# Squares folded to two tiles by VectorE before each variance, and the channel mix added to the residual by one accumulating DMA

## The reference, cut to what matters

```
cond:   y = sigmoid(x) * num / den * (0.8 + 0.2 tf)    # num, den: scans over the 512 tokens in both
                                                      # directions, keys and values from fside
attn:   h  = layernorm(y)                      # mean and variance over the 512 channels
        r, k, v = mixes of h and its shifted copy, each @ (512 x 512)
        x1 = y + (sigmoid(r) * wkv(k, v)) @ Wout
        h2 = layernorm(x1)                     # second mean and variance
        r2 = sigmoid(mix(h2) @ cWr);  k2 = relu(mix(h2) @ cWk) ** 2
        x2 = x1 + r2 * (k2 @ cWv)              # the channel mix added to the residual
x = x + x2
x = x + ffn(cond2(x))     # cond2: the same scans, gated by the new x; ffn: shared expert and 32 routed experts, top 8
```

## Time and profile before

| | |
|---|---|
| median of 3 runs | 1136.41 us (1134.61 to 1138.21) |
| the profiled execution's own time | 1126.11 us |
| its span | 1124.4 us |
| TensorE busy | 1048.5 us, 93% of the span |
| VectorE busy | 724.5 us, 64% |
| ScalarE busy | 513.0 us, 46% |
| GpSimd busy | 472.0 us, 42% |

### The profile page before, as it was taken

The page is one execution under the profiler, slowest core; times in us unless marked ns, Lnnn a source line. Parts: engine busy times, 40 slices in busy tenths (PEclk is TensorE's granted clock), DMA queues, the critical chain, the costliest instruction groups (busy, mean ns, idle before and its releaser), DMA issues.

```text
span 1124.4 us, 13091 instructions
## 1 busy us (share of the span) xinstructions
PE 1048.5 (93%) x4094; PEld 649.4 (58%) x4095; DVE 724.5 (64%) x1346; ACT 513.0 (46%) x778; POOL 472.0 (42%) x432
## 2 busy tenths in 40 slices
PE   0479999999999999999999999998999999999788
PEld 0344444444444444554644444446999999999788
DVE  8998449999999999870787000003555555555376
ACT  4465525656565556341221111113666666666211
POOL 3533003532353236220008777662666666666500
PEclk9999999999999999999999999999999999999889
DMA  4563024432643211321204685357766776677398
GB/s 149 173 213 101 1 38 138 151 101 59 204 151 101 64 39 33 101 38 75 75 1 139 216 286 191 143 174 205 161 157 157 157 156 157 157 157 157 115 405 299
DMA packets 186322, 157.23 MB, mean 140 GB/s; under 512 B 113824, under 2 KB 159392, under 8 KB 184224
## 3 DMA queue, kind: packets, MB, share of 16 engines
q1 hardware_dynamic: 170336, 113.12, 35.6%
q0 software_dynamic: 15936, 43.53, 12.3%
HBM read 67.09 MB, written 68.55 MB: 121 GB/s over the span
## 4 chain that ended last, share of the span: by engine, by line
PE 75%; DVE 17%; issue 4%; DMA 2%; ACT 1%; POOL 0%; ACTq 0%; POOLq 0%; SPq 0%; DVEq 0%
PE banks L1596 24%; PE banks L605 13%; PE banks L616 12%; PE banks L570 10%; PE banks L543 10%; PE banks L675 2%; PE banks L519 2%; DMA arena<-parts 2%; DVE arena L1345 2%; PE banks L1611 2%; DVE arena L1336 2%; DVE arena L1334 1%; DVE arena L1447 1%; DVE arena L1438 1%; PE banks L665 1%
## 5 line engine op out<-in xcount | busy, mean ns | idle before, releaser
L1596 PE MATMUL banks<-arena 128*128 128x512 f32 x896 | 389.7, 595 | 12.2 <-DVE arena L1399 5.1
L1596 PEld LDWEIGHTS banks<-arena 128*128 128x128 f32 x896 | 170.3, 191 | 228.7 <-issue 216.9
L482 POOL DMA_INDIRECT parts<-arena x160 | 171.0, 1069 | 126.4 <-DVE arena L879 101.3
L474 POOL DMA_INDIRECT slots_in<-arena x128 | 129.2, 1010 | 91.1 <-issue 87.1
L605 PEld LDWEIGHTS banks<-arena 128*128 128x128 f32 x1280 | 156.8, 194 | 7.9 <-issue 3.9
L605 PE MATMUL banks<-arena 128*128 128x128 f32 x1280 | 157.4, 277 | 3.0 <-ACT arena L713 3.0
L616 PE MATMUL banks<-arena 128*128 x640 | 151.1, 379 | 0.0
L879 DVE TENSOR_TENSOR arena<-banks,arena 128x512 f32<-128x512 f32 x80 | 55.3, 691 | 119.9 <-PE banks L616 119.9
L616 PEld LDWEIGHTS banks<-arena 128*128 128x128 f32 x640 | 115.6, 190 | 12.5
L543 PE MATMUL banks<-arena 128*128 128x512 f32 x256 | 114.3, 592 | 0.0
L570 PE MATMUL banks<-arena 128*128 128x512 f32 x256 | 114.1, 592 | 0.0
(11 more groups left out here) (179 smaller groups left out, 1239.7 us busy)
## 6 DMA issues: line engine op xcount, KB each, us to landing
slots_in<-arena SPq DMA_DIRECT2D x20, 1120.0 KB, 5.9
arena<-parts SPq DMA_DIRECT2D x16, 1024.0 KB, 10.0
arena<-fT SPq DMA_DIRECT2D x32, 256.0 KB, 2.8
arena<-w2T SPq DMA_DIRECT2D x4, 2048.0 KB, 13.6
arena<-xT SPq DMA_DIRECT2D x4, 1024.0 KB, 7.9
arena<-xT POOLq DMA_DIRECT2D x4, 1024.0 KB, 9.7
arena<-w1T SPq DMA_DIRECT2D x2, 2048.0 KB, 13.1
out<-arena SPq DMA_DIRECT2D x16, 256.0 KB, 6.9
```

The lines of the kernel that those rows point to most:

```text
L474: pool.indirect_dma_start(rows_in, bass.IndirectOffsetOnAxis(ap=POSU[:, n, j:j + 1], axis=0), XLR[:, n].bitcast(mybir.dt.uint32), None).th ...
L482: pool.indirect_dma_start(parts, bass.IndirectOffsetOnAxis(ap=DESTU[:, g:g + 1], axis=0), YO[:, i % 4, c], None).then_inc(y_sent[i % 4], 16)
L1596: ins = pe.matmul(out, w[:, k, m * P:(m + 1) * P], x[:, k], start=(k == 0), stop=(k == kt - 1))
```

## The change

Two things are changed.

1. Six of the eight variances (all four of the second layer norm, those of batches 2 and 3 of the first) get a `fold` ahead of them: one VectorE instruction adds squares tiles 2 and 3 to tiles 0 and 1 (128 x 1024 elements), and TensorE then multiplies two tiles and not four. TensorE waits for `sq{which}_folded` there and no longer for ScalarE's squares.
2. For batches 0, 1 and 2 the four instructions of `x_new` are gone from VectorE. GpSimd issues one accumulating DMA from `R2S` to `XN[:, b]` (1 MB, from SBUF to SBUF) ahead of its work for slot 7, once `final_a` is done, and ScalarE's `sig_new` waits for the DMA's semaphore `x_full`. Batch 3 keeps `x_new`.

```diff
+        def folded(which, b):
+            return which == 2 or b >= 2
...
                 for n, it in enumerate(items):
...
+                    if b is not None and n == 7:
+                        new_x(b - 1)
                     if nx is not None and not last:
                         mid(nx)
                     post(it)
...
-                if b is not None:
-                    pool.wait_ge(S['x_summed'], 16 * b)
+            def new_x(b):
+
+                pool.wait_ge(S['x_summed'], 16 * (b + 1))
+                pool.wait_ge(S['v2_evac'], 4 * b + K)
+                pool.dma_start(XN[:, b], R2S, accum_op=ALU.add).then_inc(S['x_full'], 16)
...
             def sig_new(b):
                 for m in range(K):
-                    act.wait_ge(S['xnew_ready'], 4 * b + m + 1)
+                    act.wait_ge(*((S['x_full'], 16 * (b + 1)) if b < B - 1 else (S['xnew_ready'], m + 1)))
...
+            def fold(which, b):
+
+                dve.wait_ge(S[f'sq{which}_ready'], b + 1)
+                sq = squares(which, b)
+                dve.tensor_tensor(sq[:, 0:2], sq[:, 0:2], sq[:, 2:4], ALU.add).then_inc(S[f'sq{which}_folded'], 1)
...
                 def open_second():
                     if b >= 2:
                         x_side(b - 2, 3)
+                    if b == 1:
+                        fold(2, 0)
                     product(b, 0)
                     normalise(2, b - 1)
...
                     center(1, b + 1)
+                    slot(items[6], lambda: fold(1, b + 1))
                 else:
                     slot(items[5])
-                slot(items[6])
+                    slot(items[6])
...
-                x_new_all(b - 1)
                 if nxt:
                     slot(items[7], settle_second)
+                    fold(2, b)
                 else:
...
                     bonus_num(it)
+                    fold(2, b)
                     x_sides(b - 1)
...
             def var(which, b):
                 src = squares(which, b)
-                pe.wait_ge(S[f'sq{which}_ready'], b + 1)
-                for k in range(K):
-                    ins = pe.matmul(STAT, ones, src[:, k], start=(k == 0), stop=(k == K - 1))
+                if folded(which, b):
+                    pe.wait_ge(S[f'sq{which}_folded'], folds(which, b))
+                else:
+                    pe.wait_ge(S[f'sq{which}_ready'], b + 1)
+                n = K // 2 if folded(which, b) else K
+                for k in range(n):
+                    ins = pe.matmul(STAT, ones, src[:, k], start=(k == 0), stop=(k == n - 1))
```

More of the change, by code:

```diff
@@ L208, in squares, with folds @@
             return MR if which == 1 and b != 1 else NR
+        def folded(which, b):
+            return which == 2 or b >= 2
+        def folds(which, b):
+            return b + 1 if which == 2 else b - 1
         def bank(n):
@@ L221, in build @@
             z2_ready sq2_ready mean2_done var2_done rs2_ready norm2_ready own2_ready mix2_ready mix_columns shifts_ready
+            sq1_folded sq2_folded
             r_mm k_mm v_mm o_mm r2_mm k2_mm v2_mm
             r_evac k_evac v_evac o_evac r2_evac k2_evac k2_ready v2_evac
-            x_summed
+            x_summed x_full
             xnew_ready xnew_sig xs_ready xs_stored0 xs_stored1
```

## The result

The changed kernel takes 1146.13 us (median of 5 runs, 1143.07 to 1148.84), beside 1137.79 us (1134.61 to 1138.21) of the kernel before in the same job: ratio 1.0073, 95% interval [1.0047, 1.0100]. It is slower by some 8 us. Forecast were 1135.9 us, in a range that ends at 1141.0.

The account below looks back on a forecast made before the run. A cycle's chain alternates between VectorE's piece (63.5 us) and TensorE's (48.5 us). Entry -1.42, cycles -0.26 and exit +1.14 sum to -0.5 us: 1136.41 becomes 1135.9 us, range 1131.5 to 1141.

Parts of the forecast that it names:

- The entry: Second norm of batch 0: VectorE waits for TensorE's variance there, so two matmuls fewer gain 1.42 us; its fold is free.
- The price of a fold: Each fold on VectorE was taken at 1.14 us, from the nearest row, L1438, of the same size.
- rival 1: TensorE is the bound by its sum, so all 10.3 us of removed matmuls are saved: 1126.1 us; chance 0.07.
- The fold went first and GpSimd was stopped: At both places in a slot the fold starts first; GpSimd gives up to 1.1 us, VectorE later by as much.
- The DMA was hidden in both cycles: DMA taken to land 9.7 us after issue, under 16 us of cover in a cycle, so it costs nothing.
- a sign of being wrong: ScalarE waiting for `x_full` at the exit would show the forecast wrong; the DMA's cover there was put at 12.2 us.
- The two cycles: VectorE's piece loses `x_new` (2.41 us) and gains two folds (2.28 us): -0.13 us a cycle, -0.26 us for two.
- One place can give something back: GpSimd's L1011 may stop the third of VectorE's L1474, losing up to 0.5 us of lead: +0.35 a cycle, not -0.13.
- rival 4: GpSimd stops each of five folds outside the entry by some 0.9 us: +4.5 us, 1140.4 us; chance 0.11.
- count for nothing in the sum: Matmuls removed from four variances in VectorE's piece of two cycles only lengthen TensorE's wait for L1399: no gain.
- my own forecast for the wait: TensorE's wait for L1399 in each cycle was to grow from 1.72 to about 3.6 us.
- The exit: Iteration 3: the fold ahead of `x_sides` lies on VectorE's chain and counts in full, +1.14 us (to +1.7).

Follow-up runs that it names:

- fold_only: The changed kernel without the DMA: the six folds stay and `x_new` is back on VectorE; cycles of 117.01 and 115.30 us.
- fold_early: The changed kernel with the second norm's fold moved ahead of the slot's second backward scan; 1142.7 us, ratio 1.0049 to the kernel before.
- fold_before_num: The changed kernel with the second norm's fold one instruction earlier, in front of L1377, which releases GpSimd; cycles of 111.82 and 113.43 us.
- best: The kernel before plus the DMA and only second-norm folds, in front of L1377, none at the exit; ratio 0.9987 [0.9959, 1.0016].
- early_padded: fold_early with four matmuls of each cycle issued twice, about 3.4 us of TensorE; stretch 3.5 us shorter than in fold_early.
- second_padded: second_only with four matmuls of each cycle issued twice, 3.4 us of TensorE; 1127.26 us beside 1130.66 us of second_only in the same job.
- second_only: fold_early without the first norm's folds and without the fold at the exit; 1130.66 us.

## Why the prediction was wrong

**What held.** The entry, -1.42 us, to the hundredth. The price of a fold, 1.13 us. The removed matmuls lay where TensorE waits for VectorE, so rival 1 did not come. The fold went first and GpSimd was stopped. The DMA was hidden in both cycles. At the exit ScalarE did wait for it (8.56 us to 470.99 us), which I had named as a sign of being wrong; but ScalarE then waited 5.22 us more for VectorE before the squares, so it cost nothing. What I looked for was a wait where I should have looked for a late successor.

**The step that failed first: "The two cycles", with its "One place can give something back".** I followed one collision with GpSimd, L1011 against the three L1474, and bounded it at 0.5 us; it cost 0.39. There were two more on the same stretch. The prediction had the fold stop GpSimd, "with VectorE later by as much", and took that for no cost; but GpSimd became 0.91 us later and VectorE 1.13, and this slip of 0.22 us let GpSimd's third operation stop the 128 x 2 operation (+1.00). Then L1011 of the next slot, released behind VectorE's late clip, stops the fourth L1474 (+1.11). The term was +2.09 a cycle and not -0.13. fold_only, fold_early and fold_before_num show that the fold's place makes the stop of L1352; the stop of L1494 stands in the two kernels that have the stop of L1352 (the changed one and fold_only) and in none of the others, and no experiment parts the two. "The folds are stopped by GpSimd" (rival 4) was the right fear with the wrong victim: the folds take 1.22 us in every profile and were never stopped.

**The step that failed second: the removed matmuls "count for nothing in the sum".** They are idle time of TensorE, and the clock fell behind it. In the profiles 104 records take 44.90 us behind waits of 0.28 to 1.72 us, 44.90 or 46.60 behind 1.99 to 2.00 us, and 46.46 to 47.89 us behind 3.19 to 3.24 us. The stretch of 152 at the exit takes 65.50 us up to a wait of 2.00 us, and 67.06 to 68.41 behind 3.19 us, in all six kernels that have such a wait. So one long wait ahead of TensorE's piece costs 1.6 to 3.0 us, about as much as the two matmuls that a fold removes (1.72 us) or more. The trace of before had a row that warned, outside the stretch that I read: up to 70 us TensorE is busy for only 23.36 us, so the two engines are both nearly full from 200 us on and not from the start. At 74.22 us its products start behind a wait of 4.71 us, and the window behind it stands at half clock:

```profile
74.22 32.84 PE L1596 MATMUL banks<-arena 128*128 128x512 f32 x72 [4.71 <-DVE arena L1450]
```

```profile
76.00:78.00 2.00, 2.00 (x3) 0.68 (x2) 2.00 (x5) 2.00 (x4) 0.00 (x0) 0.50 0.11 31
```

The waits of 1.7 us left the clock at 1.00, and my own forecast for the wait was 3.6 us, between the two. It should have been priced from both. The Trainium skill, page "TensorE: Matmul & The Clock Gate", section "Part 1: The HAM clock gate (the "warmup" mystery)", says that the half-rate clock is the default and that recent activity lifts it, and that it varies from run to run where the change falls. By this rule equal waits can end in either clock, and the trace agrees: 1.99 and 2.00 us in best, and 2.99 us at the exit with and without a loss. early_padded against fold_early, and second_padded against second_only, are the direct tests: matmuls added, VectorE's work unchanged, and stretches 3.5 and 3.4 us shorter. In time the second pair shows it, 3.4 us in one job with intervals apart; the first pair's 2.8 us are from two jobs with intervals that overlap.

**The exit.** The fold's +1.14 was right. The clock made it 2.4 us in this profile. Of the five kernels with this fold and a wait of 2.99 to 3.00 us behind it, four lose clock there (7.64 to 7.78 us for 24 records) and fold_before_num does not (6.09 us).

**The sum.** Forecast were -0.5 us. In the profile the path to the channel mix gained 1.42 and lost 4.18 in the cycles, 1.14 for the last fold, and 1.55 + 1.26 to the clock: +6.7. The medians differ by 8.3 us, with an interval of 5.3 to 11.4 us.

**What stays open.** Why the clock falls behind one wait of 2.0, 2.1 or 3.0 us and not behind another equal one was not settled in this case; even the profiles of before and after differ at 54 to 66 us, where TensorE's instructions are the same. It is also open why VectorE's small operation gets in ahead of GpSimd's next instruction when it comes 0.28 to 0.30 us before the running one ends, and is stopped for the whole of the next when it comes 0.06 us before; the Trainium skill, page "SBUF — State Buffer", section "Who interferes with whom", gives a lock held for a whole instruction, and the duration of 1.32 us that ends with L1029 agrees. The share of the second part was not worked on; fold_only's stretch is 2.8 us longer than the changed kernel's and its ratio lower, and the second part's scatter is large enough for that.

## What to carry to other kernels

Where two engines take turns as the chain, work removed from one while it waits is not free time: it can become one long wait in front of its own turn, and TensorE may begin that turn at 1.2 GHz. Look at the longest wait ahead of each stretch of matmuls, and if no wait of that length in the trace has a full clock behind it, price the loss; keeping the engine fed, even with repeated matmuls, can be the faster kernel.

VectorE and GpSimd are tied by phase: an instruction added behind the one that releases GpSimd delays VectorE's next instructions by its own length and GpSimd's group by another, and a slip of 0.22 us cost a stop of 1.00 us here. Follow every later collision in the cycle, not only that of the new instruction; one place earlier the same instruction may cost nothing beyond itself. And price each variant from the piece in which the engines are tied: here neither the DMA alone nor the folds alone gained. The DMA with one well-placed fold in each turn shortened the stretch by 2.6 us, and by 4.3 us with TensorE padded; only the padded one is clearly faster in time.

## What the runs showed of the hardware that was not expected

- A VectorE operation on 128 x 2 elements took 1.32 us and not 0.32, beside one GpSimd operation of 1.26 us.
- An accumulating DMA of 1 MB from SBUF to SBUF landed in 6.9 to 7.6 us, faster than the one from memory (9.1 to 10.5).
- Repeating 3.4 us of matmuls in each cycle made a kernel faster by 3.4 us (second_padded against second_only).
- TensorE's clock fell to 1.2 GHz behind a wait as short as 1.99 us (best, at 288.96), though its timeline shows no wait from 178.55 to 286.97.
